# Interleaving the pair products of a DLRM tower more finely with its other matmul work

## The reference

```python
e = jnp.stack([tbl_0[ids[:, 0]], ..., tbl_25[ids[:, 25]]], axis=1)
combined = jnp.concatenate([dense[:, None, :], e], axis=1)            # 2048 x 27 x 128
interactions = jnp.einsum('bnd,bmd->bnm', combined, combined)
z = jnp.concatenate([dense, interactions[:, _TRIU_I, _TRIU_J]], axis=1)
h = jnp.concatenate([z, dense], axis=1)                               # 607 columns
h = jnp.maximum(h @ W_top1 + b_top1, 0.0)                             # 512
h = jnp.maximum(h @ W_top2 + b_top2, 0.0)                             # 256
y = h @ W_top3                                                        # 1
```

## Time and profile before

| what | value |
|---|---|
| runs | 370.5, 372.38, 372.94 us; median 372.38 |
| profiled execution | span 373.1 us (0.7 above the median) |
| PE matmuls | busy 332.0 us, 89% of the span |
| POOL | busy 258.6 us, 69%; 272 gathers |
| DVE, ACT | 207.1 us (55%), 188.8 us (51%) |
| mean granted TensorE clock | 0.977 |

### The profile page before, as it was taken

How to read it: one execution, slowest core, us unless ns; L and a number is a source line. 1 busy time by engine, 2 the same in 40 slices (tenths; PEclk the granted TensorE clock), 3 DMA queues, 4 the chain that set the end, 5 groups by cost and what they waited for, 6 DMA issues and landing times.

```text
span 373.1 us, 13491 instructions
## 1 busy us (share of the span) xinstructions
PE 332.0 (89%) x6048; PEld 298.5 (80%) x6048; DVE 207.1 (55%) x375; ACT 188.8 (51%) x223; POOL 258.6 (69%) x280
## 2 busy tenths in 40 slices
PE   0377859899999899998999999999999999999895
PEld 0377848898799778996789978998799878997685
DVE  3799745694089703874059912885079704860030
ACT  2698462455545473553635564554645563556402
POOL 6777777777777777777777777777777777776000
PEclk9997898899999999998999999999999999999999
DMA  7999426772226622464215722464226622442230
GB/s 178 246 259 212 135 79 174 193 229 69 55 68 151 198 53 59 95 194 125 58 54 128 233 54 58 93 192 131 58 59 150 205 54 57 105 116 62 51 40 21
DMA packets 49332, 44.24 MB, mean 119 GB/s; under 512 B 33359, under 2 KB 39094, under 8 KB 49274
## 3 DMA queue, kind: packets, MB, share of 16 engines
q1 hardware_dynamic: 39166, 25.36, 26.9%
q0 software_dynamic: 8704, 17.84, 18.2%
q10 hardware_dynamic: 1404, 0.17, 0.3%
HBM read 37.91 MB, written 5.44 MB: 116 GB/s over the span
## 4 chain that ended last, share of the span: by engine, by line
PE 82%; DMA 5%; issue 5%; ACT 4%; DVE 2%; SPq 1%; ACTq 1%; DVEq 0%
PE banks L443 38%; PE banks L462 14%; PE mlp L481 13%; PE moved L426 8%; PE mlp L491 7%; DMA w_sb<-in_tbl_dram 3%; DVE masks L672 1%; ACT vectors L818 1%; ACT hidden L846 1%; PE mlp L502 1%; SPq L250 1%; ACTq L229 1%; DMA scratch<-products 1%; DMA features<-scratch 1%; DVE low L659 1%
## 5 line engine op out<-in xcount | busy, mean ns | idle before, releaser
L401 POOL DMA_INDIRECT rows<-in_tbl_dram,ids_sb x272 | 257.7, 948 | 84.0 <-issue 80.8
L672 DVE TENSOR_TENSOR masks<-hot_ids,row_of 125x512 fp32r<-125x512 int32 (+1 forms) x336 | 185.6, 619 | 93.7 <-PE banks L443 84.8
L443 PE MATMUL banks<-masks,high 125*128 125x256 f32 x592 | 154.3, 298 | 17.4 <-DVE low L659 17.4
L443 PE MATMUL banks<-masks,low 125*128 125x256 f32 x592 | 150.3, 291 | 0.0
L443 PEld LDWEIGHTS banks<-masks,high 125*128 125x128 f32 x592 | 118.9, 201 | 18.1 <-issue 15.2
L443 PEld LDWEIGHTS banks<-masks,low 125*128 125x128 f32 x592 | 119.1, 201 | 0.0
L818 ACT ACTIVATE vectors<-moved 128x512 f32<-128x512 f32 (+1 forms) x80 | 86.8, 1085 | 4.6 <-PE moved L426 4.3
L801 ACT ACTIVATE vectors<-banks 128x512 f32<-128x512 f32 (+1 forms) x40 | 44.4, 1111 | 77.4 <-PE banks L443 77.4
L462 PEld LDWEIGHTS banks<-vectors 128*27 128x27 f32 x4096 | 44.5, 104 | 24.7 <-issue 19.6
L462 PE MATMUL banks<-vectors 128*27 128x27 f32 x4096 | 54.1, 193 | 9.7 <-issue 5.0
L481 PE MATMUL mlp<-features,w_sb 117*128 117x256 f32 x224 | 54.6, 388 | 0.0
(11 more groups left out here) (46 smaller groups left out, 64.4 us busy)
## 6 DMA issues: line engine op xcount, KB each, us to landing
hot_ids<-in_ids_of_field_dram SPq DMA_DIRECT2D x32, 256.0 KB, 4.9
rows<-in_tbl_dram,ids_sb POOLq DMA_INDIRECT x272
features<-scratch SPq DMA_DIRECT2D x7, 351.0 KB
scratch<-products SPq DMA_DIRECT2D x56, 42.2 KB
scratch<-products SPq DMA_DIRECT2D x28, 81.2 KB
w_sb<-in_tbl_dram SPq DMA_DIRECT2D x3, 448.0 KB
hot_ids<-in_ids_of_field_dram SPq DMA_DIRECT2D x8, 128.0 KB
dense_sb<-in_dense_dram SPq DMA_DIRECT2D x8, 128.0 KB, 5.2
```

The lines of the kernel that those rows point to most:

```text
L401: pool.indirect_dma_start(rows[:, (tile * TILE_ROWS + v) % RING, :], None, tables[f][:, :], bass.IndirectOffsetOnAxis(ap=ids_sb[:, tile, f ...
L443: last = nc.tensor.matmul(banks[:, j % BANKS, m * CHUNK:(m + 1) * CHUNK], part[:, part_of(j * PAIR + m, k), :], masks[:, mask % MASK_RING, ...
L672: nc.vector.tensor_tensor(masks[:, mask % MASK_RING, 0:size], hot_ids[0:PART_ROWS, n % ID_RING, 0:size], row_of[0:PART_ROWS, row:row + 1]. ...
```

## The change

A pair step can be done in two visits of 8 groups (32 matmuls of the source, 64 records, 64 weight loads) each. Only the second visit signals that the step is ready, and only the first has the step's waits. In `end_of_chunk` a visit stands where a whole step stood, and the other visit one slot later: step 0 around turn 0 and a first layer tile; step 1 around turn 2, the fourth first layer tile and turn 3; steps 2 and 3 around parts of the next chunk's first lookup (parts 0 to 2, 3 and 4, 5 to 7). Chunk 0 splits steps 2 and 3 alone; the last chunk splits step 2 around half a second layer tile and keeps step 3 whole. ACT copies step 0 after the second tile's batch 0, and step 1 after batch 3. DVE, POOL and SP have the order they had.

```diff
+VISITS = 2
+VISIT_GROUPS = STEP_GROUPS // VISITS
...
-            def look_up(c, j):
+            def look_up(c, j, ks=None):
+                ks = ks or range(PARTS[j])
...
-                elif j < BANKS:
+                elif j < BANKS and ks[0] == 0:
...
-                for k in range(PARTS[j]):
+                for k in ks:
...
-            def multiply(c, s):
-                if s == 0:
+            def multiply(c, s, visits=range(VISITS)):
+                for visit in visits:
+                    multiply_part(c, s, visit)
+
+            def multiply_part(c, s, visit):
+                if s == 0 and visit == 0:
...
-                for g in range(STEP_GROUPS):
+                for g in range(visit * VISIT_GROUPS, (visit + 1) * VISIT_GROUPS):
...
-                last.then_inc(step_ready, 1)
+                if visit == VISITS - 1:
+                    last.then_inc(step_ready, 1)
...
-                multiply(LAST, 2)
-                second_layer(LAST - 1, 1)
+                multiply(LAST, 2, (0,))
+                second_layer(LAST - 1, 1, range(0, 2))
+                multiply(LAST, 2, (1,))
+                second_layer(LAST - 1, 1, range(2, MTILES1))
...
             def end_of_chunk(i):
                 b = TILES * i + 1
                 first_layer(i - 1, 0)
-                multiply(i, 0)
+                multiply(i, 0, (0,))
                 turn(b, 0)
                 first_layer(i - 1, 1)
-                multiply(i, 1)
+                multiply(i, 0, (1,))
                 turn(b, 1)
                 first_layer(i - 1, 2)
+                multiply(i, 1, (0,))
                 turn(b, 2)
                 first_layer(i - 1, 3)
                 turn(b, 3)
+                multiply(i, 1, (1,))
                 second_layer(i - 1, 0)
                 turn(b, 4)
                 if i < LAST:
                     second_layer(i - 1, 1)
-                    multiply(i, 2)
-                    look_up(i + 1, 0)
-                    multiply(i, 3)
+                    multiply(i, 2, (0,))
+                    look_up(i + 1, 0, range(0, 3))
+                    multiply(i, 2, (1,))
+                    look_up(i + 1, 0, range(3, 5))
+                    multiply(i, 3, (0,))
+                    look_up(i + 1, 0, range(5, PARTS[0]))
+                    multiply(i, 3, (1,))
...
                 keep_first(i - 1, 0)
-                keep_step(i, 0)
                 keep_batch(b, 0)
                 keep_first(i - 1, 1)
-                keep_step(i, 1)
+                keep_step(i, 0)
                 keep_batch(b, 1)
                 keep_first(i - 1, 2)
                 keep_batch(b, 2)
                 keep_first(i - 1, 3)
                 keep_batch(b, 3)
+                keep_step(i, 1)
                 keep_second(i - 1, 0)
```

More of the change, by code:

```diff
@@ L428, in turn @@
                 last.then_inc(batch_ready, 1)
-            def look_up(c, j):
+            def look_up(c, j, ks=None):
+                ks = ks or range(PARTS[j])
                 if c == 0:
                     pe.wait_ge(low_made, PAIR * j + WIDTHS[j])
-                elif j < BANKS:
+                elif j < BANKS and ks[0] == 0:
                     pe.wait_ge(step_kept, (c - 1) * CHUNK_STEPS + j + 1)
-                if j >= BANKS:
+                if j >= BANKS and ks[0] == 0:
                     pe.wait_ge(pair_kept, c * HOT_PAIRS + j - BANKS + 1)
-                for k in range(PARTS[j]):
+                for k in ks:
                     mask = c * MASKS + FIRST_MASK[j] + k
@@ L453, in multiply @@
                     pe.wait_ge(dense_placed, c + 1)
-                if s == TILE_STEPS:
+                if s == TILE_STEPS and visit == 0:
                     pe.wait_ge(batch_kept, (c + 1) * CHUNK_BATCHES)
                 t, of_step = divmod(s, TILE_STEPS)
-                for g in range(STEP_GROUPS):
+                for g in range(visit * VISIT_GROUPS, (visit + 1) * VISIT_GROUPS):
                     at = of_tile(c * TILES + t) + (of_step * STEP_GROUPS + g) * QUADS
@@ L483, in first_layer, with second_layer @@
                 last.then_inc(first_ready, 1)
-            def second_layer(c, m):
+            def second_layer(c, m, ks=range(MTILES1)):
                 if c < 0:
@@ L489, in second_layer @@
                     pe.wait_ge(first_kept, MTILES1 * (c + 1))
-                for k in range(MTILES1):
+                for k in ks:
                     last = nc.tensor.matmul(mlp[:, m, 0:CHUNK], w2_sb[:, k, m * 128:(m + 1) * 128], hidden1[:, k, :],
                                             start=(k == 0), stop=(k == MTILES1 - 1))
-                last.then_inc(second_ready, 1)
+                if MTILES1 - 1 in ks:
+                    last.then_inc(second_ready, 1)
             def last_layer(c):
@@ L593, in first_chunk @@
                 turn(1, 4)
-                multiply(0, 2)
-                look_up(1, 0)
-                multiply(0, 3)
+                multiply(0, 2, (0,))
+                look_up(1, 0, range(0, 3))
+                multiply(0, 2, (1,))
+                look_up(1, 0, range(3, 5))
+                multiply(0, 3, (0,))
+                look_up(1, 0, range(5, PARTS[0]))
+                multiply(0, 3, (1,))
             def second_chunk():
```

## The result

| kernel | median | runs | against before |
|---|---|---|---|
| before | 371.44 us | 4, 370.31 to 372.94 | |
| change | 375.74 us | 4, 374.09 to 377.13 | 1.0131 [1.0079, 1.0182] |
| change, measured again | 377.14 us | 12 | 1.0102 [1.0065, 1.0138] |

The forecast of 370.8 us and its range up to 374.2 both missed. The profiled execution of the change has a span of 374.9 us and took 376.67 us, 1.8 more than its span.

The account below looks back on a forecast made before the run. PE's order was taken to set the pace, POOL's gathers a close second bound. About 10 us won up to the last turn 3 is cut off at 2.4; span 373.1 - 1.6 = 371.5, less 0.7: 370.8 us, range 369.0 to 374.2.

Parts of the forecast that it names:

- POOL's floor: Last chunk: turn 3 must wait for rows POOL gathers, so it starts at 344.0 instead of 346.35, however much PE gains.
- Visits pay on PE: All chunks up to the last turn 3: splitting pair steps into visits saves PE about 10 us, bounds -2 and +15.
- Order of the tail up to step 3: Last chunk from turn 3: next pair step at 348.2, an instruction stall until 354.0, step 3's end at 354.3 instead of 355.97.
- no less than 3.7 us: Last chunk's pair steps: least time for a packet's worth of PE instructions; 3.73 set the stall's end at 354.0.
- Half 0 usable at 355.6: Half 0's DRAM round trip: step 1 copied at 346.6, plus 6.4 to the load and 2.6 until usable; PE waits 1.3 us.
- Half 0's work of 7.5 us: PE's work on half 0 after its load: takes 7.5 us and ends at 363.1.
- the fall of the clock: Rival, chance 0.25: half clock right behind turn 3 in the tail makes the second layer tile 1.6 us longer, giving 372.4.
- If that 0.6 is gone, each us of lateness is a us of time: Tail: half 1's data, at 363.7, come 0.6 us after half 0's work ends, so half 0's lateness is just covered.
- the forecast 7.8 us: End of the kernel: time from half 1's data at 363.7 to the end of the span at 371.5.
- Half 1, which was forecast to be last: Half 1's DRAM round trip: 9.37 us from step 3's end, data at 363.7, the later of the two halves by 0.6.
- Minus 0.7 to come from the span to the median: Last term of the sum: the median of the runs lies 0.7 below the profiled span, so 371.5 becomes 370.8 us.
- The stalls for instructions: Pair steps: PE waits for instruction packets (1.5 to 1.8 us seen before); step 3 should be stalled once.

Follow-up runs that it names:

- e1: The change, but with steps 0 and 1 of the last chunk whole and in their old places: 372.07 us, 0.9998 of before.
- e5: The change plus 7 matmuls whose result nobody uses, put into PE's wait for half 0: 375.25 us, 1.0092 of before.
- e6: The change, with ACT issuing half of half 0's 12 writes instead of SP issuing all: 373.34 us, 1.0045 of before.
- e9: The change itself, unedited, measured and traced once more: 377.14 us, 1.0102 of before.
- e11: The change, but in the last chunk step 1 is whole, right behind step 0's second visit and ahead of turn 1: 372.35 us, 1.0002 of before.
- e12: The kernel of e1 (last chunk's steps 0 and 1 whole in their old places), measured once more: 371.82 us, 0.9989 of before.
- e16: The change with half 0's writes shared between SP and ACT, and 4 unused matmuls behind step 3: 373.62 us, 1.0013 of before.
- e7: The change, with all last-chunk steps whole and layer tiles moved ahead of turns that wait for rows; steps 2 and 3 adjacent: 373.61 us, 1.0058 of before.
- e10: The kernel before, unedited, measured again with 12 runs and a trace: 372.96 us, 1.0011.
- e8: The kernel of e7 with half 0's writes also shared between SP and ACT: 375.43 us, 1.0073 of before.
- e3: The kernel before without the 17th table's gathers from chunk 1 on (14 left out; output not the reference's): 366.21 us, 0.9827 of before.

## Why the prediction was wrong, point by point

- **POOL's floor: right.** Turn 3 came at 343.34 against a forecast of 344.0, and at 343.2 to 343.8 in the change, e1, e5, e6, e9, e11 and e12; 344.61 where the last gather was late (e16).
- **Visits pay on PE: right in direction, too high in size.** Without 14 of the gathers it is 5 to 8 us, where about 10 were forecast (the sum there writes 1.6 for a term worked out as 1.8). A visit is longer than I had it: in the 58 visits of the change's trace that stand alone the mean from the first record to the next piece is 0.82 us, median 0.86, where 0.63 and an exit of 0.10 were set. This did not decide the time, as the floor cuts the gain off at 3.0 us.
- **Order of the tail up to step 3: right.** First pair step behind turn 4 at 347.5 (348.2), one stall of 1.15 us (1.5), end 353.5 (354.3). The "no less than 3.7 us" for a packet's worth of instructions is not a floor: it was 3.45 in e7.
- **Half 0 usable at 355.6: the step that failed.** It was 357.45. Step 1's copy was even early (over by 346.0; forecast 346.6), but the way from the copy to the load took 8.3 us instead of 6.4, and the load 3.1 instead of 2.6. I had carried over 5.20 for the 12 issues, and they took 7.16, with the difference in two of them. The old stretch had no packet of PE's instructions and the new one has two, which overlap just those two issues; that they are the cause is likely and not shown. The forecast had a wait of 1.3 us here; it was 3.88.
- **Half 0's work of 7.5 us: failed with it.** It took 9.6, as PE's wait of 3.88 brought 1.2 GHz; 7.70 at full clock (e5), so that 0.2 of it was a misreading. I had the fall of the clock as a rival, but priced it behind turn 3 and not behind the wait for half 0 that I had myself put into the forecast. The Trainium skill's rule ("TensorE: Matmul & The Clock Gate", HAM oscillation), that bursts behind waits start slow, is borne out at this wait: 3.88 and 4.03 us, and 2.03 in e6, were followed by 0.50, and 0.79 in e5 was not. Nor was the wait of 1.12 ahead of turn 3 in the change (1.00 from 344 to 349).
- **"If that 0.6 is gone, each us of lateness is a us of time": right, and it decided.** Half 0's work ends at 367.06 instead of 363.1: 1.85 from lateness and 2.1 from its own length. From there to the end it took the forecast 7.8 us: 374.9. Half 1, which was forecast to be last, had its data in time.
- **Minus 0.7 to come from the span to the median: a wrong term.** A run takes 1.8 us more than its span (376.67 for 374.9 here, 375.11 for 373.3 in e10), so the profiled execution of before was one of about 374.9 us, 2.5 above the median with which it was compared (372.38). I had noted a distance of 0.7 and took it to hold for the changed kernel as well. A span of 371.5 is 373.3 us of time. By the table of traces, what such an execution has above the median is mostly PE's lateness at turn 3, the same that the floor cuts off. So even with half 0 in time there was little or nothing to win: e1's and e11's kernels show it, 1.000 of before.
- **The sum of the misses.** The span came out 3.4 us above the forecast (half 0's lateness of 1.85 and its longer work of 2.1, less the 0.6 that half 1 had left), the step from span to time was 2.5 too low, and the profiled execution was 0.9 above its median: 5.0, for the 4.9 between 370.8 and 375.74.
- **The stalls for instructions: right.** The rule of the Trainium skill ("Runtime: NRT & Kernel Launch", Instruction fetch mechanics) that crossing a block is mostly hidden was weighed against the earlier trace rows and left out of the sum. The traces do not agree with it for this kernel: 1.15 us in step 3 of the change, and 1.54 and 1.84 in e7, where nothing stands between two pair steps.

## What to carry to other kernels

A step that starts a round trip through DRAM should be placed by when the data are wanted at the other end, and not by what the step costs on its engine. Before, half 0 had 4 us to spare. In the change its data came 5.4 us later and PE was ready for them 2.5 us earlier, and the rest was a wait of 3.9. Such a wait can cost more than its length: with the clock's fall behind it, half 0's work took 1.4 us more in e6 (a wait of 2.03) and 1.9 more in the change.

The same interleaving is harmless where the result is wanted a chunk later, so an order that is good in the loop deserves its own look in the last iteration. And before a gain is promised from one trace, ask whether that execution is a typical one: span and time of the same execution first, then the median.

## What the runs showed of the hardware

- **Slow DMA issues coincide with packets of the instruction queue.** SP's writes of half 0, from the view of one line (ns min/median/max), before and in the change:

```profile
L229 SPq DMA_DIRECT2D scratch<-products x12: 318/391/424, 343.0 to 347.8; - x12
```

```profile
L231 SPq DMA_DIRECT2D scratch<-products x12: 317/392/1501, 346.0 to 352.8; - x12
```

  The two long ones, 1.27 us at 346.36 and 1.50 at 350.77, start in the two packets of the instruction queue from 346.2 to 347.2 and from 350.5 to 351.8; before had none in that stretch. In the traces of before, the change (twice) and e1's kernel (twice), 36 of the 38 issues of `products` that took 1.05 us or more (up to 2.04) overlap such a packet, and 74 of the 502 shorter ones. That the one makes the other was not tried by itself.
- **Where PE had to wait for it, a packet's worth of instructions took 3.5 to 3.7 us.** From one stall's end to the next, 256 or so instructions later: 351.94 to 355.67 before, 349.92 to 353.65 in e8, 350.12 to 353.57 in e7. A pair step of 256 runs in 1.1 us without a break, so by these rows it needs some 2.5 us of other work beside it (an estimate).
- **The breaks inside pair steps come with the gathers.** The same step of 128 records, in before while POOL gathers and in e3 9 us after its last gather:

```profile
340.12 1.61 PE L462 MATMUL banks<-vectors 128*27 128x27 f32 x128
```

```profile
333.20 1.27 PE L463 MATMUL banks<-vectors 128*27 128x27 f32 x128
```
